# A decoder layer on one core: the expert layer computed on sorted rows in tiles of 128 instead of on all tokens with all experts

## The reference

```python
x = x + attention(layernorm(x), Wq, Wk, Wv, Wo)
x = x + cross_attention(layernorm(x), ctx, mask, Wq, Wkv, Wout, bout)
h = layernorm(x)                                  # expert layer
probs = softmax(h @ Wg)                           # 8192 tokens, 8 experts
top_vals, top_idx = top_k(probs, 2)
gates = top_vals / sum(top_vals)
expert_out = einsum('th,ehd->etd', h, We) + be
x = x + sum(gates * expert_out[top_idx, token])
```

## Time and profile before

| | |
|---|---|
| median of three runs | 3581.41 us (3578.99 to 3582.03) |
| span of the profiled execution | 3581.8 us |
| PE busy | 3501.3 us, 98% |
| DVE busy | 2358.7 us, 66% |
| ACT busy | 2220.8 us, 62% |
| POOL busy | 2121.2 us, 59% |
| bytes moved by DMA | 47.44 MB, mean 13 GB/s |

### The profile page before, as it was taken

The page is one execution under the profiler, slowest core; times in us unless marked ns, Lnnn a source line. Parts: engine busy times, 40 slices in busy tenths (PEclk is TensorE's granted clock), DMA queues, the critical chain, the costliest instruction groups (busy, mean ns, idle before and its releaser), DMA issues.

```text
span 3581.8 us, 80997 instructions
## 1 busy us (share of the span) xinstructions
PE 3501.3 (98%) x28992; PEld 2949.8 (82%) x28992; DVE 2358.7 (66%) x7401; ACT 2220.8 (62%) x6442; POOL 2121.2 (59%) x1928
## 2 busy tenths in 40 slices
PE   6899999999999999999999999999999999999998
PEld 5788888888888888888888888888888888888886
DVE  6666667666666666676666666666766667666665
ACT  5666666666666666666666666666666666666663
POOL 5555676555665556765556755566655567555662
PEclk8999999999999999999999999999999999999999
DMA  3100000000000000000000000000000000000000
GB/s 98 37 10 13 10 10 10 10 13 12 7 10 12 9 12 10 9 10 10 12 12 7 10 12 10 12 10 9 10 10 12 12 7 12 11 10 12 13 6 8
DMA packets 46796, 47.44 MB, mean 13 GB/s; under 512 B 8256, under 2 KB 43328, under 8 KB 46400
## 3 DMA queue, kind: packets, MB, share of 16 engines
q1 hardware_dynamic: 45696, 41.99, 4.0%
q10 hardware_dynamic: 704, 0.27, 0.0%
HBM read 33.86 MB, written 8.39 MB: 12 GB/s over the span
## 4 chain that ended last, share of the span: by engine, by line
PE 89%; DVE 5%; ACT 2%; issue 2%; POOL 2%; DMA 0%; ACTq 0%; POOLq 0%; DVEq 0%
PE unit_ps L536 19%; PE pT_ps L648 14%; PE oT_ps L665 14%; PE score_ps L632 11%; PE unit_ps L524 10%; PE wo_ps L690 10%; PE unit_ps L546 8%; DVE x L1021 1%; ACT probs L798 1%; POOL probs L1150 1%; DVE probs L936 1%; PE unit_ps L555 1%; DVE bn L863 1%; DVE x_in L1029 1%; ACT v_sb L744 1%
## 5 line engine op out<-in xcount | busy, mean ns | idle before, releaser
L1150 POOL TENSOR_TENSOR probs<-probs,inv_sum 128x512 f32<-128x512 f32 x1024 | 1062.1, 1041 | 956.4 <-DVE inv_sum L919 956.3
L787 ACT ACTIVATE pT<-pT_ps 128x512 f32<-128x512 f32 x1024 | 606.2, 594 | 136.1 <-PE pT_ps L648 135.5
L798 ACT ACTIVATE probs<-probs,neg_max 128x256 f32<-128x256 f32 x1024 | 508.9, 500 | 276.4 <-DVE probs L936 276.4
L648 PE MATMUL pT_ps<-ident,probs 128*128 128x128 f32 x4096 | 634.0, 279 | 13.2 <-POOL probs L1150 12.5
L648 PEld LDWEIGHTS pT_ps<-ident,probs 128*128 128x128 f32 x4096 | 451.8, 141 | 221.8 <-issue 204.0
L798 ACT ACTIVATE probs<-score_ps,neg_max 128x256 f32<-128x256 f32 x1024 | 476.6, 476 | 179.1 <-DVE neg_max L925 179.1
L665 PE MATMUL oT_ps<-pT,v_sb 128*64 128x256 f32 x4096 | 556.0, 392 | 4.4 <-ACT pT L787 4.0
L936 DVE TENSOR_SCALAR_CACHE_REDUCE probs<-score_ps,mask_add 128x256 f32<-128x256 f32 x1024 | 433.4, 480 | 104.8 <-PE score_ps L632 101.9
L536 PE MATMUL unit_ps<-xs_hi,w_lo 128*128 128x256 f32 x1536 | 460.1, 300 | 9.3 <-DVE swap L972 7.8
L536 PE MATMUL unit_ps<-xs_hi,w_hi 128*128 128x256 f32 x1536 | 436.6, 284 | 0.0
L536 PE MATMUL unit_ps<-xs_lo,w_hi 128*128 128x256 f32 x1536 | 436.1, 284 | 0.0
(11 more groups left out here) (121 smaller groups left out, 8573.0 us busy)
## 6 DMA issues: line engine op xcount, KB each, us to landing
x_in<-dram_x SPq DMA_DIRECT2D x32, 256.0 KB, 2.7
xn<-dram_ctx SPq DMA_DIRECT2D x32, 256.0 KB, 2.7
layer_out<-x SPq DMA_DIRECT2D x32, 256.0 KB, 2.2
swap<-dram_bout SPq DMA_DIRECT2D x32, 128.0 KB, 3.1
rope<-dram_be SPq DMA_DIRECT2D x32, 64.0 KB, 2.9
rope<-dram_we SPq DMA_DIRECT2D x5, 256.0 KB, 2.8
probs<-dram_sk SPq DMA_DIRECT2D x4, 256.0 KB, 5.1
x<-dram_cq SPq DMA_DIRECT2D x4, 256.0 KB, 3.2
```

What stands on the lines that cost most here:

```text
L648: last = nc.tensor.transpose(pT_ps[s % 2][:, k * T + t * P:k * T + (t + 1) * P], probs[:, hs % P_BUFS, t, k * P:(k + 1) * P], ident[:])
L787: nc.scalar.activation(flat(pT[:, s % 2, :, :]), pT_ps[s % 2][:], ACT.Copy).then_inc(pT_ready.sem, 1)
L798: last = nc.scalar.activation(dst, src, ACT.Exp, bias=neg_max[:, h % STATS, t:t + 1], scale=1.0 if h < H else -1.0, accum_out=row_sum[:, h ...
L1150: nc.gpsimd.tensor_tensor(weights, weights, inv.unsqueeze(2).to_broadcast([P, NT, T]), ALU.mult).then_inc(probs_ready.sem, 1)
```

## The change

The eight dense EX units per sequence go. In their place the tokens of a group of sequences are sorted by expert in DRAM and each expert is applied to its own rows only.

- Sorting. DVE's gate table now also makes one-hot rows and running counts (g_hot, g_here, g_past). A new unit RK in slot 11 multiplies them with a triangular matrix, which gives each token its place within its expert. DVE turns that into row numbers (rows). In slot 13 POOL scatters the normalized rows of the sequence, once per choice, into x_rows in DRAM by four indirect DMAs (128 rows of 1 KB each).
- Tiles. The sequences form five groups of 9, 9, 8, 4 and 2. When a group is complete, DVE lists its tiles of 128 rows with their experts (list_tiles). Tiles are taken in pairs, (4 n + 8) / 2 pairs for n sequences: 22, 22, 20, 12 and 8, 84 in all. For each pair SP reads row and expert from the list into registers and loads two tiles of rows (128 KB each) and two experts' weights (512 KB each). PE transposes the rows (unit TT, 4 transposes) and multiplies (unit TM, 12 matmuls of 256 columns). ACT and DVE split the transposed rows, ACT copies the result to y_tile, SP stores it to y_all.
- Sums. For each sequence and each half of it POOL gathers the two chosen results per token by two indirect DMAs, and DVE adds them, weighted, to x1, which went to DRAM and was loaded back (add_half). SP stores the output.
- Schedule. Pairs run in bodies 10 to 17 and 19 to 32: none in bodies 0 to 9 and 18, two in 16, 17, 25 and 26, three in 10 to 15 and 19 to 24, five in 27 to 32. Ten pairs are left for after body 32. The first three pairs of a body stand in slots 8 to 14, the fourth and fifth in the drain. Sums run in bodies 18 to 25 and 27 to 32, 26 of them, six after the last body. Their gathers stand in slots 0 and 4 for the first sum of a body, 8 and 12 for the second, 20 and 24, 28 and 32.
- Setup. In bodies 0, 2, 4 and 6 SP writes zeros over x_rows and y_all (19456 rows of 1 KB, four times). The split expert weights are stored to DRAM in body 0.

```diff
-GATE_STEPS = 8
+GATE_STEPS = 12
...
+GROUPS = ((0, 9), (9, 18), (18, 26), (26, 30), (30, 32))
...
+PAIRS_IN = {**{b: (0, 3) for b in range(10, 16)}, 16: (0, 2), 17: (0, 2),
+            **{b: (1, 3) for b in range(19, 25)}, 25: (1, 2), 26: (1, 2),
+            27: (2, 5), 28: (2, 5), 29: (2, 5), 30: (2, 5), 31: (3, 5), 32: (3, 5)}
+SUMS_IN = {18: 2, **{b: 1 for b in range(19, 26)}, 27: 2, 28: 2, 29: 3, 30: 2, 31: 4, 32: 4}
+GATHER_AT = (0, 4, 8, 12, 20, 24, 28, 32)
...
-    8: [("V", 2, 0, LATE), ("EX", 0, -1, LATE)],
-    9: [("EX", 1, -1, LATE)],
+    8: [("V", 2, 0, LATE), ("TT", 0, 0, NOW)],
+    9: [("TM", 0, 0, LATE)],
     10: [("V", 3, 0, NOW)],
-    11: [],
-    12: [("EX", 2, -1, NOW)],
-    13: [],
-    14: [("EX", 3, -1, NOW)],
+    11: [("RK", 0, -1, LATE), ("TT", 1, 0, NOW)],
+    12: [("TM", 1, 0, LATE)],
+    13: [("TT", 2, 0, NOW)],
+    14: [("TM", 2, 0, LATE)],
     15: [],
     16: [],
-    17: [("K", 4, 0, NOW), ("EX", 4, -1, NOW)],
-    18: [("GT", 0, -1, NOW), ("EX", 5, -1, NOW), ("EX", 6, -1, LATE), ("V", 4, 0, NOW), ("L2", 0, 0, LATE)],
-    19: [("K", 5, 0, NOW), ("Q", 4, 0, NOW), ("EX", 7, -1, NOW)],
+    17: [("K", 4, 0, NOW), ("TT", 3, 0, NOW)],
+    18: [("GT", 0, -1, NOW), ("TM", 3, 0, NOW), ("TT", 4, 0, NOW), ("V", 4, 0, NOW), ("L2", 0, 0, LATE)],
+    19: [("K", 5, 0, NOW), ("Q", 4, 0, NOW), ("TM", 4, 0, NOW)],
...
+            def row_at(n, i):
+                at = tile_of_pair(n) + i
+                return sp.value_load(tile_list[at:at + 1, group_of_pair(n), 0:1], min_val=0, max_val=ROWS - P)
...
+            def load_pair(n):
+                g = group_of_pair(n)
+                sp.wait_ge(list_ready, g + 1)
+                if n >= 2:
+                    sp.wait_ge(tiles_done, n - 1)
+                for i in range(2):
+                    at = tile_of_pair(n) + i
+                    sp.dma_start(x_tile[:, n % 2, i, :],
+                                 x_rows[g % 2][bass.ds(row_at(n, i), P), :]).then_inc(x_tile_in[n % 2], 16)
+                    expert = sp.value_load(tile_list[at:at + 1, g, 1:2], min_val=0, max_val=E - 1)
...
+                                 we_all[bass.ds(expert, 1), :, :].rearrange("e p n -> p (e n)")) \
+                        .then_inc(w_tile_in[n % 2], 16)
...
+            def store_pair(n):
+                g = group_of_pair(n)
+                if g >= 2:
+                    sp.wait_ge(half_done, NT * GROUPS[g - 2][1])
+                sp.wait_ge(y_ready, n + 1)
+                for i in range(2):
+                    sp.dma_start(y_all[g % 2][bass.ds(row_at(n, i), P), :], y_tile[:, i, :]).then_inc(y_stored[g % 2], 16)
+            def load_x1(q):
+                sp.wait_ge(stored.sem, stored.at(q, 0, 1))
+                if q:
+                    sp.wait_ge(out_stored, 16 * q)
+                sp.dma_start(x1_back[:], x1_all[q].rearrange("(t p) d -> p t d", p=P)).then_inc(x1_back_in, 16)
+            def store_sum(q):
+                sp.wait_ge(half_done, NT * (q + 1))
+                sp.dma_start(out_d[q].rearrange("(t p) d -> p t d", p=P), x1_back[:]).then_inc(out_stored, 16)
...
+                    for i in range(len(SUMS.get(b, ()))):
+                        if s == GATHER_AT[2 * i]:
+                            load_x1(SUMS[b][i])
+                    for i, n in enumerate(PAIRS.get(b, ())):
...
+                            store_pair(n)
+                            if n + 2 < pairs_through(group_of_pair(n)):
+                                load_pair(n + 2)
+                    if s == LIST_AT + 2 and b < B:
+                        first_pairs(b)
+                    for i in range(len(SUMS.get(b, ()))):
+                        if s == min(GATHER_AT[2 * i + 1] + 3, SLOTS - 1):
+                            store_sum(SUMS[b][i])
...
+            for n in LAST_PAIRS:
+                if n - 2 >= LAST_PAIRS[0]:
+                    store_pair(n - 2)
+                if group_of_pair(n) == len(GROUPS) - 1:
+                    load_pair(n)
+            for n in LAST_PAIRS[-2:]:
+                store_pair(n)
+            for n in LAST_SUMS:
+                load_x1(n)
+                store_sum(n)
+            sp.wait_ge(out_stored, 16 * B)
...
+            def pair_turns(ps, n):
+                pe.wait_ge(x_tile_in[n % 2], 32 * (n // 2 + 1))
+                turn(ps, x_tile[:, n % 2, :, :]).then_inc(tiles_turned, 1)
+            def pair_products(ps, n):
+                pe.wait_ge(tile_lo_ready, n + 1)
+                pe.wait_ge(w_tile_in[n % 2], 32 * (n // 2 + 1))
+                for i in range(2):
...
+                        for a, half in ((xf_lo, 1), (xf_hi, 0), (xf_hi, 1)):
+                            last = nc.tensor.matmul(ps[:, i * D:(i + 1) * D], a[:, c, i * P:(i + 1) * P],
+                                                    w[:, half, :], start=k == 0, stop=k == 3 * NC - 1)
...
+                last.then_inc(tiles_done, 1)
...
+                elif kind == "RK":
...
+                    pe.wait_ge(gate_step.sem, gate_step.at(b, off, GATE_STEPS))
+                    flat_here, flat_past = flat(g_here[:]), flat(g_past[:])
+                    nc.tensor.matmul(ps[:, 0:(NT + 1) * E], below[:], flat_here, start=True, stop=False)
+                    nc.tensor.matmul(ps[:, 0:(NT + 1) * E], ones[:], flat_past, start=False,
+                                     stop=True).then_inc(rank_done.sem, 1)
+                elif kind == "TT":
+                    pair_turns(ps, PAIRS[b][g])
                 else:
-                    j, t = divmod(g, NT)
-                    tile_product(ps[:], t, we_hi, we_lo, 2 * j * D, 2 * D).then_inc(expert_done.sem, 1)
...
+            pe.wait_ge(bias_added.sem, bias_added.at(B - 1, 0, 1))
+            pe.wait_ge(rank_read.sem, rank_read.at(B - 1, 0, 1))
+            pe.wait_ge(y_ready, LAST_PAIRS[0])
+            for n in LAST_PAIRS:
+                pe.wait_ge(tile_lo_ready, n)
+                pair_turns(unit_ps[0], n)
+                pe.wait_ge(y_ready, n)
+                pair_products(unit_ps[1], n)
...
+            def tile_high(ps, n):
+                act.wait_ge(tiles_turned, n + 1)
+                nc.scalar.activation(flat(xf_hi[:]), ps, ACT.Copy).then_inc(tile_hi_ready, 1)
+            def tile_out(ps, n):
+                act.wait_ge(tiles_done, n + 1)
...
+                    act.wait_ge(*pairs_stored(n - 1))
...
+                nc.scalar.activation(flat(y_tile[:]), ps, ACT.Copy).then_inc(y_ready, 1)
...
+                share = share_of[:, b + off, :, :]
+                nc.vector.tensor_tensor(share, g_top[:, :, 0:2], g_rtwo[:].to_broadcast([P, NT, 2]),
                                         ALU.mult).then_inc(gate_step.sem, 1)
-                dve.wait_ge(gate_step.sem, gate_step.at(b, off, 6))
+                iota = iota_sb[:].unsqueeze(1).unsqueeze(1).to_broadcast([P, NT, 2, E])
+                nc.vector.tensor_tensor(g_hot[:], iota, g_idf[:, :, 0:2].unsqueeze(3).to_broadcast([P, NT, 2, E]),
+                                        ALU.is_equal).then_inc(gate_step.sem, 1)
+                dve.wait_ge(gate_step.sem, gate_step.at(b, off, 7))
+                if b + off:
+                    dve.wait_ge(rank_done.sem, rank_done.at(b, off - 1, 1))
+                nc.vector.tensor_tensor(g_part[:], g_hot[:], share.unsqueeze(3).to_broadcast([P, NT, 2, E]), ALU.mult)
+                nc.vector.tensor_tensor(g_here[:, 0:NT, :], g_hot[:, :, 0, :], g_hot[:, :, 1, :],
+                                        ALU.add).then_inc(gate_step.sem, 1)
+                if (b + off) in [begin for begin, _ in GROUPS]:
...
+                dve.wait_ge(gate_step.sem, gate_step.at(b, off, 9))
+                nc.vector.tensor_tensor(gates[:], g_part[:, :, 0, :], g_part[:, :, 1, :],
+                                        ALU.add).then_inc(gate_step.sem, 1)
                 for t in range(NT):
...
-                                                       g_val[:, t, i:i + 1], ALU.is_equal, ALU.mult)
-                last.then_inc(gate_step.sem, 1)
-                dve.wait_ge(gate_step.sem, gate_step.at(b, off, 7))
-                nc.vector.tensor_tensor(gates[:], g_first[:], g_second[:], ALU.add).then_inc(gate_step.sem, 1)
...
+            def tile_low(ps, n):
+                dve.wait_ge(tile_hi_ready, n + 1)
+                low_part(xf_lo[:], ps, xf_hi[:]).then_inc(tile_lo_ready, 1)
+            def add_half(q, t):
+                dve.wait_ge(x1_back_in, 16 * (q + 1))
+                dve.wait_ge(y_rows_in, 32 * (NT * q + t + 1))
+                x1_t = x1_back[:, t, :]
+                nc.vector.scalar_tensor_tensor(x1_t, y_rows[:, 0, :], share_of[:, q, t, 0:1], x1_t,
+                                               ALU.mult, ALU.add).then_inc(half_step, 1)
+                dve.wait_ge(half_step, NT * q + t + 1)
+                nc.vector.scalar_tensor_tensor(x1_t, y_rows[:, 1, :], share_of[:, q, t, 1:2], x1_t,
+                                               ALU.mult, ALU.add).then_inc(half_done, 1)
```

(27 more changed lines are left out.)

320 lines of the change are left out of this document (252 added, 68 removed).

## The result

The changed kernel takes 4070.3 us (median of 4 runs, 4057.8 to 4074.0) against 3581.6 for the kernel before: ratio 1.136, interval 1.134 to 1.138. The direction was forecast, the size was not: 489 us slower, where the prediction had 229 and its range ended at 3960.

The account below looks back on a forecast made before the run. PE, busy 98%, was taken as the bound, with a second bound just behind it almost everywhere. Terms 0 + 0 + 40 + 44 + 5 + 140 = 229 us on the profiled 3581.8 gave 3811 us, range 3680 to 3960.

Parts of the forecast that it names:

- as long as before: Sign to look for in the trace after: bodies 1 to 9 keep their length of 109 us.
- 3 to 6 us longer: Sign to look for in the trace after: bodies with pairs and sums grow by 3 to 6 us.
- the drain: Last self-attention values to first cross-attention scores: chain and clock take what missing EX work gives; 0 us, bounds 31 either way.
- slots 8 to 13 without pairs: Bodies 1 to 9 and 18: EX units leave, and by slot 13 PE is about 0.8 us early.
- Rival C: Slots 8 to 19 of 31 bodies: PE's 211 us come back in full, faster than before, 3511 us; chance 8%.
- the price X of an indirect DMA: Scatters between heads 12 and 13, and gathers: each indirect DMA holds POOL for 0.70 us, with 0.38 and 1.30 kept.
- rival A: POOL's issues are dear: each indirect DMA holds it for 1.3 us, 3940 us; chance 25%.
- bodies with pairs: Slots 8 to 15 of 21 bodies: head 13 is ready 1.9 us late; 40 us, from 12 to 90.
- gathers: 22 sums before body 32, their gathers on POOL, dearest in slots 0 and 4: 44 us, bounds 21 and 86.
- the end: Behind the last projection: sums and pairs hang on single buffers, 140 us after the old end, bounds 105 and 185.
- the start: Clearing 80 MB in bodies 0, 2, 4 and 6: 5 us, bounds 0 and 20.
- B: Only the end costs; POOL takes scatters and gathers in its idle time, PE's slots stay as long: 3712 us; chance 22%.

Follow-up runs that it names:

- b_no_ex: The kernel before with all eight EX units (dense expert work) left out of every body: 3518.8 us, ratio 0.983.
- a_pair_end: The changed kernel with three pairs of a body moved to slots 13, 17 and 18 and two pairs to 17 and 18: 4134.2 us.
- a_idle: The changed kernel with scatters at slot 16, first pairs of a sequence at slot 28 and gathers mostly moved to slots 19 to 29: 3931.2 us.
- a_tail_const: The changed kernel, but pairs behind the last body take a fixed expert's weights instead of one read from the list, bytes unchanged: 4064.6 us.

## Why the prediction was wrong

The step that failed is the price of an indirect DMA on POOL, 0.70 us where the runs show 1.27, and with it the assumption that a wait on PE costs only its own length. The signs that I had named say so too: bodies 1 to 9, "as long as before", are 3.4 us longer (6.5 while rows are cleared), and bodies with pairs and sums, "3 to 6 us longer", take 10.7 us more (19 to 24) and 23.8 (27 to 31).

**Right within its bound: the drain.** Term 0, bound 31: measured 12.6 us against 13.3, 20 us gained in 31 bodies. The rows of body 0 were the right place to read it from. They are the kind with the lower clock in it (13.4); most bodies have it elsewhere and take 12.1 to 12.4, which is the gain.

**Right: slots 8 to 13 without pairs, and that PE's time would not come back.** "By slot 13 PE is about 0.8 us early": measured 0.7. b_no_ex shows 0.8 per body in the same slots. Rival C, faster, is refuted: without any expert work the kernel gains 60 us, not 211.

**Wrong: the price X of an indirect DMA, the step on which most terms hung.** I took 0.70 us, from an instruction with hardly any data; it is 1.27, and 3.0 to 5.8 in the bodies where the descriptor area is full. My own high end, 1.30, was within 0.03, and rival A, built on it, had 3940: that is half of the 259 us that my sum lacked. But even so it had 2.2 us per body without pairs and 22 in all. Measured are 48 us in those ten bodies (slots 8 to 19), 9 of them through clearing. What the step lacked beside X is the clock: I used its drop in the drain and did not apply it to the wait that I reckoned with here. In body 8 it adds up: 3.6 us of wait, 2.5 of slower transposes, projections and values behind it (5.1 us at half speed), less 1.4 of EX and 0.1 of a shorter drain, 4.6 us, where this body's slots 14 to 19 grew by 4.5.

The Trainium skill (DMA: Bandwidth & Descriptors, Specifications) has about 1 us for GpSimd's DMAs, as latency to the first byte. In this trace the first packet of an indirect DMA starts 1.5 us or more (median 1.7) after POOL's instruction begins and 0.6 or more (median 0.7) after it ends. What POOL is held for, 1.27 us, is another quantity. My sum with 1 us, 65 us higher, would have been nearer, but by luck.

**Mis-sized: bodies with pairs.** 40 us predicted (12 to 90), 119 measured: 75 in the 16 bodies with two or three pairs and 44 in the five with five. The part through slot 11 was right (1.55 us late predicted, 1.5 measured), but not as reckoned, and so in part by luck: I had PE wait 0.6 and 1.0 us for the transposes of heads 8 and 9; in bodies 10 to 17 these waits are 0.4 us together, and 1.0 us stands in front of the first pair's own products. Missing were slots 12 and 13 (another 1.5 us, 2.3 with five pairs), where I took a pair for as good a filler as an EX unit. It isn't. In slots 8 to 13 PE has no waits over 0.1 us in the kernel before, 2.8 us of them in the changed kernel's bodies without pairs, and still 2.2 us in bodies 10 to 17: the pairs' work comes on top of these waits instead of filling them. a_pair_end shows the same from the other side, 3.6 us per body. The rest stands in slots 14 to 19 and is X and the clock again.

**Mis-sized: gathers, 44 predicted (21 to 86), 91 measured in slots 0 to 7 alone.** The step had 2.8 us less 0.4 for the two halves in each of 13 bodies, 31 us. With X at 1.27 it gives 5.1 less 0.4, 61 us for these bodies; measured are 6.7 to 7.5 per body (in bodies 19 to 24 2.3 for the first half and 4.4 for the second, which the lower clock follows). a_idle takes 90 of 97 us away by place.

**Mis-sized: the end, 140 predicted (105 to 185), 194 measured.** The sums were nearly right (11.8 us predicted, 12.7 measured; the six take 79 instead of 71). Pairs take 7.6 us, not the 5.4 by bytes; what paces them stays open, see a_tail_const. And the five pairs of body 32, which share SyncE's queue with its four sums, were left out, so that the sums end 76 us behind the last projection and not 45. Bytes at a queue's best rate were the wrong end to take the value from; "pairs of 8 us" stood in my bounds.

**Not seen at all:** SyncE's queue. In body 27 the two pairs of the drain keep it for 14 us before x1's store (3249.2 to 3263.5); slots 20 to 35 of bodies 27 to 31 lose 38 us, 35 of them to this queue.

**Mis-sized: the start.** 5 predicted, about 9 measured, nearly all in the scatters of bodies 2, 4 and 6; they are the 9 us named under X.

Rival A (3940) had the right mechanism and too small a size, because it left the clock and the queue out and the tail 39 us too short. B is refuted by the six bodies that have neither pairs nor sums nor clearing: they are 3.4 us longer each on average.

## What to carry to other kernels

Price the instruction by how long it holds its in-order engine, and put it where that engine is idle: the same four DMAs cost 4 us between two heads and nothing three slots later. Where units fill waits, removing them gives back less than their time (here a sixth), and what replaces them should be as free of dependencies. A wait that you predict on PE may have to be charged twice, once for itself and once for the clock behind it (here 3.6 and 2.5 us); and whatever is added to a DMA queue is added ahead of all that stands behind it.

## What the runs showed of the hardware

- An indirect DMA of 128 rows of 1 KB holds POOL for 0.94 to 1.21 us (median 0.97) and the next starts 0.30 later, scatter or gather alike.
- With 1024 bytes for descriptors a pause of 2.0 to 2.4 us stands before some indirect DMAs, mostly seven or eight apart or a multiple of that, with 512 mostly before every third or fourth; 3.9 to 6.3 us in bodies 2, 4 and 6, where clearing keeps the DMA engines busy (328 GB/s around the pause of body 2). It ends 0.5 to 0.6 us after the DMA directly before has landed.
- After a wait of 3.6 us PE ran at 1.2 GHz until 5.1 us after it. Bodies with the same work have drains of 12.2 or 13.2 us, according to whether a stretch at 1.2 GHz falls into them.
- A register load on SyncE from SBUF adds 0.7 us to the issue of 0.4 behind it (1.12 us from one issue to the next instead of 0.40).
